# Two blocks of W1 in one load, half of a product step ahead of four transposes, and ten small VectorE operations moved

## What is computed

```python
x = x + base(x, W_base) + lora0(x; Wt, A, B_w, Wp, scaling)[idx 0..3]   # per sequence
x = x + x @ W.T + (x @ A1[i].T @ B1[i].T) * s1[i]                       # i in 0..6
x = x + einsum('bct,bcd->bdt', x, w2[j])                                # 64x64 mix over tokens
x = x + einsum('bct,bcd->bdt', x, w3[k])                                # 64x64 mix over tokens
```

## Time and profile before

| | |
|---|---|
| median of 3 runs | 167.16 us (167.01 to 167.16) |
| the profiled execution, its own time | 168.06 us |
| its span, first to last instruction | 166.3 us |
| PE busy | 161.5 us, 97% |
| DVE busy | 92.2 us, 55% |
| POOL busy | 57.5 us, 35% |
| ACT busy | 47.2 us, 28% |
| mean DMA rate | 185 GB/s |

### The profile page before, as it was taken

The page is one execution under the profiler, slowest core; times in us unless marked ns, Lnnn a source line. Parts: engine busy times, 40 slices in busy tenths (PEclk is TensorE's granted clock), DMA queues, the critical chain, the costliest instruction groups (busy, mean ns, idle before and its releaser), DMA issues.

```text
span 166.3 us, 6376 instructions
## 1 busy us (share of the span) xinstructions
PE 161.5 (97%) x2365; PEld 125.6 (75%) x2365; DVE 92.2 (55%) x220; ACT 47.2 (28%) x90; POOL 57.5 (35%) x167
## 2 busy tenths in 40 slices
PE   5999999999999999999999999999999999999993
PEld 5788738767786868886877887788778886887783
DVE  4856865689877394357726843783484345333011
ACT  3135124573215204220322213122402420422110
POOL 4261120354541269227404820490067007500000
PEclk9999999999999999999999999999999999999999
DMA  4899994658844824569834822683076321433113
GB/s 146 267 371 317 275 267 163 174 210 292 285 149 170 282 102 130 187 181 364 280 132 145 313 96 78 215 289 126 7 269 231 126 91 48 119 126 130 65 63 126
DMA packets 21949, 30.80 MB, mean 185 GB/s; under 512 B 7273, under 2 KB 9705, under 8 KB 21929
## 3 DMA queue, kind: packets, MB, share of 16 engines
q1 hardware_dynamic: 20320, 25.31, 45.7%
q0 software_dynamic: 1600, 5.24, 10.1%
q10 hardware_dynamic: 8, 0.00, 0.0%
HBM read 19.80 MB, written 10.75 MB: 184 GB/s over the span
## 4 chain that ended last, share of the span: by engine, by line
PE 97%; POOL 1%; issue 0%; ACT 0%; POOLq 0%
PE o_ps L872 70%; PE y_ps L872 21%; PE o_ps L917 2%; PE y_ps L956 1%; PE y_ps L885 1%; PE y_ps L925 1%; PE y_ps L931 0%; PE y_ps L969 0%; PE y_ps L1000 0%; ACT o_sb L577 0%; POOL ident L376 0%; POOL piece L373 0%; PE y_ps L934 0%; POOL ident L371 0%; POOL owner L374 0%
## 5 line engine op out<-in xcount | busy, mean ns | idle before, releaser
L872 PE MATMUL o_ps<-g,yy 128*128 128x512 f32 (+1 forms) x384 | 89.0, 389 | 0.0
L872 PEld LDWEIGHTS o_ps<-g,yy 128*128 128x128 f32 x384 | 70.5, 188 | 20.3 <-issue 5.3
L408 POOL COPY u_sel<-u_tab 128x64 f32 x128 | 32.4, 273 | 60.6 <-PE o_ps L872 40.1
L740 DVE TENSOR_TENSOR yy<-y_all,yy 128x512 fp32r<-128x512 f32 x32 | 22.2, 698 | 25.6 <-ACT yy L500 25.4
L500 ACT ACTIVATE yy<-y_all 128x512 fp32r<-128x512 f32 x32 | 20.1, 629 | 51.1 <-PE o_ps L872 23.7
L780 DVE COPY o_sb<-o_ps 128x512 f32<-128x512 f32 x15 | 10.4, 691 | 22.0 <-PE o_ps L872 15.4
L733 DVE COPY y_all<-y_ps 128x512 f32<-128x512 f32 x32 | 19.9, 682 | 3.8 <-PE y_ps L872 3.8
L396 POOL DMA_INDIRECT v_sel<-v_table,v_rows x16 | 15.5, 967 | 10.9 <-PE o_ps L872 7.5
L532 ACT ACTIVATE o_sb<-o_ps 128x512 f32<-128x512 f32 x16 | 9.4, 591 | 21.5 <-PE o_ps L872 17.6
L769 DVE COPY w_sel<-w2T 64x64 f32 x56 | 11.4, 215 | 4.8 <-issue 2.3
L872 PE MATMUL o_ps<-g,wb 128*128 128x512 f32 x48 | 13.4, 424 | 0.0
(11 more groups left out here) (121 smaller groups left out, 118.5 us busy)
## 6 DMA issues: line engine op xcount, KB each, us to landing
out_dram<-o_sb SPq DMA_DIRECT2D x14, 512.0 KB
x_odd<-in_x_dram SPq DMA_DIRECT2D x12, 512.0 KB
x_even<-in_x_dram SPq DMA_DIRECT2D x4, 512.0 KB
w_sb<-in_L_cond_W_dram SPq DMA_DIRECT2D x4, 256.0 KB, 5.3
wb_sb<-in_L_cond_W_base_dram SPq DMA_DIRECT2D x4, 256.0 KB, 5.8
wp_sb<-in_L_cond_Wp_dram SPq DMA_DIRECT2D x2, 512.0 KB, 7.8
wt_sb<-in_L_cond_Wt_dram SPq DMA_DIRECT2D x1, 1024.0 KB, 9.9
w_of<-v_tab SPq DMA_DIRECT2D x4, 256.0 KB, 3.2
```

What stands on the lines that cost most here:

```text
L408: nc.gpsimd.tensor_copy(u_sel[2 * h + u][:, :, b, RANK * part:RANK * part + RANK], u_tab[:, :, bass.ds(e, 1), :].rearrange("p k a r -> p k ...
L740: nc.vector.tensor_tensor(yy[u][:, :, 1, :], y_all[u][:, :, :], yy[u][:, :, 0, :].bitcast(F32), ALU.subtract).then_inc(yl_set, 1)
L872: return nc.tensor.matmul(dst, lhsT, rhs, start=start, stop=stop)
```

## The change

The order of PE is changed in one place, two loads become one (with a tensor `w1_rest` for blocks 2 and 3 and a helper `w1_block` that finds a block), and `find_row_shift` is called after `w2T` instead of after ident2.

```diff
-        w1_sb = sb("w1_sb", [PART, KC, KC, PART], of=first)
+        w1_sb = sb("w1_sb", [PART, 2, KC, PART], of=first)
+        w1_rest = sb("w1_rest", [PART, KC, D - 2 * PART], of=first)
...
+        def w1_block(k, c):
+            return w1_sb[:, k, c, :] if k < 2 else w1_rest[:, c, PART * (k - 2):PART * (k - 1)]
...
-            for k in range(KC):
-                sp.dma_start(w1_sb[:, k, :, :], w1_rows[:, k, :, :]).then_inc(w1_in[k], 16)
-                if k < 2:
-                    load_wb(k)
+            for k in range(2):
+                sp.dma_start(w1_sb[:, k, :, :], w1_rows[:, :, PART * k:PART * k + PART]).then_inc(w1_in[k], 16)
+                load_wb(k)
+            sp.dma_start(w1_rest[:, :, :], w1_rows[:, :, 2 * PART:]).then_inc(w1_in[2], 16)
...
             for k in range(KC):
-                pool.wait_ge(w1_in[k], 16)
-                blk = w1_sb[:, k, k, :]
+                pool.wait_ge(w1_in[min(k, 2)], 16)
+                blk = w1_block(k, k)
...
-            find_row_shift()
             dve.wait_ge(wb_in[0], 16)
...
                 read("w2T", w2T[SEQ * b:SEQ * b + SEQ, :, :].rearrange("p g (a j) -> p g a j", j=W2J), w2_bank, eye, ALU.add)
+            find_row_shift()
             low_wb(3)
...
             g01_high()
+            g01_step(0, range(0, 2))
             flip_w1(1)
-            g01_step(0)
+            g01_step(0, range(2, KC))
```

More of the change, by code:

```diff
@@ L161, in build @@
         a1_in = sem("a1_in")
-        w1_in = [sem(f"w1_in{k}") for k in range(KC)]
+        w1_in = [sem(f"w1_in{k}") for k in range(3)]
         wb_in = [sem(f"wb_in{k}") for k in range(KC)]
@@ L255, in _ @@
         def _(sp):
-            w1_rows = w1.rearrange("(c p) (k d) -> p k c d", p=PART, d=PART)
+            w1_rows = w1.rearrange("(c p) d -> p c d", p=PART)
             wb_rows = w_base.rearrange("(c p) d -> p c d", p=PART)
@@ L925, in flip_w1 @@
                     last = nc.tensor.transpose(bank_of(f"g1_{k}")[:, PART * c:PART * c + PART],
-                                               w1_sb[:, k, c, :], ident[:, :])
+                                               w1_block(k, c), ident[:, :])
                 last.then_inc(setup_ps, 1)
@@ L930, in _ @@
             for c in range(1, KC):
-                last = nc.tensor.transpose(bank_of("g1_0")[:, PART * c:PART * c + PART], w1_sb[:, 0, c, :], ident[:, :])
+                last = nc.tensor.transpose(bank_of("g1_0")[:, PART * c:PART * c + PART], w1_block(0, c), ident[:, :])
             last.then_inc(setup_ps, 1)
             pe.wait_ge(w1_plus, 1)
-            nc.tensor.transpose(bank_of("g1_0d")[:, 0:PART], w1_sb[:, 0, 0, :], ident[:, :]).then_inc(setup_ps, 1)
+            nc.tensor.transpose(bank_of("g1_0d")[:, 0:PART], w1_block(0, 0), ident[:, :]).then_inc(setup_ps, 1)
             keep_warm(3)
             g01_high()
+            g01_step(0, range(0, 2))
             flip_w1(1)
-            g01_step(0)
+            g01_step(0, range(2, KC))
             pe.wait_ge(ids_f_set, 2 + 5)
```

## The result

The changed kernel takes 168.09 us (median of 8 runs, 167.71 to 168.70) against 167.18 us for the kernel before (8 runs, 167.01 to 167.95). The ratio is 1.004, with a 95% interval of 1.0023 to 1.0057. By the medians it is slower by 0.9 us, where 0.89 us was forecast (168.05 against 167.16). The ratio says 0.7 us (0.0040 x 167.2), with 0.4 to 1.0 us by its interval.

What follows compares the result with a forecast made beforehand. PE was taken to bound the kernel (97% of the chain); 0.74 us at `low_wb(3)` plus 0.16 us from step 1 gave 0.90 us, 167.16 + 0.90 = 168.06, taken as 168.05 us, range 167.2 to 168.6.

Steps and rivals of the forecast that it cites:

- The path: From w2T through `low_wb(3)`, copies and `v0T` to `cross`: DVE work added there delays PE, +0.90 us in all.
- No slack: DVE between 21.3 and 27.7 us: anything added comes out on PE, which waits about 0.2 us for DVE at `cross`.
- The row shift's 0.74 us: Behind w2T: ten linked operations take 1.82 us, 1.15 us of idle time hides part, `low_wb(3)` starts 0.74 us later.
- The half step's 0.16 us: At step 1: block 1's transposes start 0.94 us later, `low_wb(1)` ends at 11.05 us, PE's weights come 0.16 us later.
- The load's 0: One load for blocks 2 and 3: PE's transposes at 10.56 us still served, cost 0; upper bound +0.7 us.
- The sum: At `cross`: weights load at 29.16 instead of 28.26 us, +0.90 us in all, with step 1's 0.16 us contained.
- The signs: Right if `low_wb(1)` ends near 11.05, `v0T` near 29.0, idle at `cross` about 1.0 us; wrong if DVE's copy idle shrinks.
- (a): Behind w2T: faster start while W_base 3 lands unchanged hides the ten; loss 0.1 to 0.3 us, 167.35 us; chance 0.14.
- (b): At block 2's transposes: merged load late, wait 0.7 us instead of step 1's 0.16; total 168.6 us; chance 0.08.
- (c): Behind w2T: port lock beside POOL's W_base 3 addition holds the first row-shift operation, +0.26 us, 168.3 us; chance 0.12.

Runs made afterwards that it cites:

- the twin: Changed kernel with only the row shift moved, to right behind the copy of `spread` instead of behind w2T, measured against the kernel before: ratio 1.0006 (0.9987 to 1.0025).

## Why the prediction was right

**The path.** The ten operations cost where the forecast put them: on the way w2T, `low_wb(3)`, copies, `v0T`, `cross`. With one row shift behind w2T four traces show PE idle at `cross` for 0.43 to 0.78 us, with the profile naming `v0T` in two of them, and the eight experiments with the row shift elsewhere have 0.04 us or none there. Moving the ten away restores the time (1.0006 against 1.0036). Behind `cross` PE takes 137.9 to 138.3 us in every trace but the one whose clock fell, so a delay at `cross` reaches the end. That is shown, by ratios and by rows.

**"No slack".** This was true of the traced execution and not of the kernel. In seven of the eight traces with the row shift elsewhere, the low part of `v0T` ended 0.48 to 0.70 us before `cross` loaded its weights; only one has 0.11 us, as the trace before had 0.12. What took the slack away in those two was the second code's load: it took 1.11 us before and 1.12 us there, and 0.31 us in four of the seven.

**The row shift's 0.74 us.** Between the trace before and that of the changed kernel `low_wb(3)` came 0.73 us later. The pitch of 0.186 us was right (20.15 to 21.83 us is nine pitches of 0.187). But the two executions differ in more than the change. Against the twin with the ten behind `spread`, counted from the start of step 1 (10.66 and 10.94 us), `low_wb(3)` comes 11.08 instead of 9.82 us behind it. That is 1.26 us later and not 0.74, since the idle stretch that takes up part of the ten is 0.64 us there and not 1.15. On the way to `cross` the twin has 1.04 us to spare: 0.46 us in which DVE waits for ACT, and 0.58 us from the end of `v0T` to `cross` (0.70 less the 0.12 that a release takes). And the code load was 0.45 us slower in the changed kernel's trace (idle 1.09 for 0.64). 1.26 - 1.04 + 0.45 = 0.67 us, which is the idle stretch that PE shows. The same sum, taken from the twin's 9.82 us and 0.64 us, fits the others within 0.05 us:

| trace | `low_wb(3)` behind step 1 | idle ahead of the last copies | worked out | PE idle at `cross` |
|---|---|---|---|---|
| before | 10.32 us | 1.44 | 0.26 | 0.28 |
| row shift alone | 11.05 | 0.86 | 0.41 | 0.43 |
| the same again | 11.09 | 0.80 | 0.39 | 0.43 |
| half step and load, no row shift behind w2T | 10.04 | 1.45 | -0.01 | 0.04 |
| changed kernel | 11.08 | 1.09 | 0.67 | 0.67 |
| the same again | 11.31 | 0.97 | 0.78 | 0.78 |

So the term came out near its size because three deviations nearly cancel: that is luck. Of its price at the end, the runs with it alone measured 0.16% and 0.31%, which is 0.3 and 0.5 us: the interval of the second, 0.1 to 0.9 us, holds 0.74, but the point is lower.

**The half step's 0.16 us.** Its arrival was right at its place, shown in the run where the clock rose as late as in the trace before. But it is not a term of the whole: alone it measured 1.0004. DVE's idle time ahead of `low_wb(3)` takes it up if the row shift is not there. In the changed kernel's trace it did not add either, since w2T ended at 20.12 us, as before, on an earlier clock.

**The load's 0.** Right in the median (0.9994). W_base 3 reached POOL at 19.86 instead of 20.14 us, but that is no effect of the merged load that could be told: it came at 18.97 to 20.14 us in the eight traces with separate loads and at 19.18 to 20.06 in the six with the merged one. The merged blocks came so late in one trace that PE lost 0.84 us. What I missed is that an addition of POOL can hold `low_wb(1)` for 0.28 us, with either kind of load.

**The sum.** The 0.89 us forecast against 0.9 us measured owes much to luck: the interval is 0.4 to 1.0 us, the ratios of the two measurements of this kernel say 0.7 and 0.6 us, and the parts measured one by one, 0.3 to 0.5 for the row shift and about 0 for each of the others, add to less. By the table, the two traces of the changed kernel wait longer at `cross` than the two with the row shift alone because of slower code loads (0.76 and 0.65 us for 0.54 and 0.47) and, in one, 0.20 us beside POOL. Both change from one execution to the next; whether the other two edits make them more frequent is not shown.

**The signs.** The forecast's own list came out mixed. `low_wb(3)` did not wait for ACT, the idle stretch at `cross` grew, and from there both traces run in step. But `low_wb(1)` ended at 10.88 us and not near 11.05, the low part of `v0T` at 28.51 and not near 29.0, and the stretch grew to 0.67 and not to about 1.0 us. One of its signs of being wrong came: the idle stretch of DVE's copies shrank, from 1.44 to 1.09 us. Read strictly, the trace did not confirm the sum of 0.90 us; the ratios and the twin confirm the path.

**The rivals.** (a), the ten hidden in an execution that starts faster, did not happen, but not for the reason given against it. Without the row shift `cross` does not wait until 28.14 us in such an execution: three traces have it at 27.49 to 27.64 us. What (a) had wrong is that W_base 3 stays at 20.14 us. It came at 19.09 to 19.33 us in these three, so DVE's idle stretch ahead of `low_wb(3)` was 0.53 to 0.64 us, and the ten took 1.86. (b) occurred in one trace of another kernel. (c), the lock beside POOL, cost little in the changed kernel's first trace: the first of the ten ran at 20.15 to 20.33 us beside POOL's addition of 19.86 to 20.32 and took 0.18 instead of 0.16 us. In its second trace the third of the ten, at 20.18 us beside POOL's addition of 20.06 to 20.52, took 0.35 instead of 0.15 us. `low_wb(1)` lost 0.28 us in the same way. The Trainium skill (SBUF — State Buffer, "Who interferes with whom") says that the shared port pair is an exclusive lock and that the order of issue decides who blocks. The traces agree in both orders: `low_wb(1)`, with two SBUF inputs, was issued at 9.92 us while POOL worked until 10.34, and took 0.28 us longer; where it was issued first, at 9.64 us, POOL's two additions took 0.34 us longer.

**What the forecast read wrongly.** It took the clock's rise at 7.5 us and the code load's 1.44 us of idle time from one trace as if they belonged to the kernel. Both change from one execution to the next, and with them the slack of the chain and the idle time in which the ten could hide.

## What to carry to other kernels

An idle stretch on an engine that is not the bottleneck hides work only up to the next place where the bottleneck waits for that engine: compare the work with the stretch, follow what is queued behind it, read both stretch and slack in more than one execution, and look for a wait that the profile calls "issue" a tenth of a microsecond behind an operation's end. An idle stretch that ends in the release of a PSUM bank is not free, even if the result that is late is needed much later. Where single executions differ by more than the effect, a trace shows who waits for whom and a ratio over many runs shows the price; neither stands in for the other.

## What the runs showed of the hardware

- PE's step from the pitch of 0.43 us to that of 0.23 us (128x512 matmuls, 1.2 and 2.4 GHz) at the start came at different times in executions of nearly the same program. The eight matmuls from 5.63 us took 2.30, 2.40, 2.43, 2.58 (twice), 3.02 and 3.24 us in the seven traces that have them in one group. The granted clock in the profile's rows was 1.00 throughout.
- A wait of PE of 1.43 us at `cross` was followed by a granted clock of 0.50 in the stretches from 30.4 to 33.4 us; the waits of up to 0.84 us in the other traces had none such behind them.
- The load of the second code by DVE's sequencer took 0.31 to 1.12 us and left the engine idle for 0.64 to 1.45 us, with the same instructions around it.
- VectorE operations with two SBUF inputs lost time beside a POOL addition that had started first: a 32x1 operation 0.3 us (0.44 for 0.15) and a 128x512 subtraction 0.3 us (0.96 for 0.68). Where the subtraction had started first, two POOL additions took 1.21 for 0.87 us.
